# Three stages in one kernel: token weights split under the image attention, the next batch's statistics and first transposes inside the last attention round, projections ahead of half the gates and of the downs

## Chip, cores and metric
One NeuronCore of a Trainium2 chip runs the whole program. The time is the device time of one execution in microseconds (us). Before the change it is 1532.42 us, the median of three runs (1531.77 to 1536.89).

## What is computed
Four images of 256 channels and 32x32 places (1024 tokens of 256) go through three blocks:

```python
x = conv_block(x)            # group norm, 1x1 q, k, v; softmax(q k^T / 16) v over 1024 places; 1x1 p; + x
t = tokens(x)                # (4, 1024, 256)
t = t + attn_block(ln(t))    # rms norm, q and k on the hyperbolic ball (atanh, tanh), v linear,
                             # 8 heads, causal softmax of -|q-k|^2 / sqrt(32), o, residual;
                             # rms norm, silu(gate) * up, down, residual
t = t + moe(ln(t))           # 8 experts, 2 a token, 256 -> 1024 -> 256, gelu
x = from_tokens(t)
```

Every matmul with a 16-bit operand is made of three: weights and activations are split into an fp16 high part and an fp16 rest ("high" and "low"), and high x high, high x low and low x high are summed (`split_product`).

## The kernel before
**Image attention** (`conv_attention`, L282). 32 steps, one for a block of 128 queries: 8 for each of 4 images. In step n TensorE computes the scores of block n (`scores`, L385) and the weighted sum of block n-3 (`weighted`, L397); for images 1 to 3 the projections ("units") come between. VectorE takes the row maximum and forms the low part of the probabilities (L540), ScalarE the exponential (L463) and the high part (L468). SyncE transposes both parts by DMA into four slots (L346, L348), behind them in each step it issues a fill of the routing table with blank rows (L350; 34 fills in all, 32 of them of 1056 KB), and every fourth step a store of the result (L339). GpSimd (POOL) only adds a bias to the input of each image (L507). The token block begins when every queue of this one is done, the fills and stores among them.

**Token block** (`token_block`, L607). Four batches. The front of a batch: layer norm statistics and factors (`statistics`, `norm_factors`, `normalised`), four pairs of transposed token tiles (`h_turned`, `h_high`, `h_low`) with one buffer for the transposed pair and one PSUM bank, the projections to q, k, v tile by tile (`qkv`, `qk_copy`, `v_copy`), the chain of small steps to the ball and to tanh (`length_roots`, `onto_ball`, `logs`, `log_factor`, `qk_roots`, `tangent_length`, `tanhs`, `factors`), then scaling, splitting and stacking q and k into a tile (`scale_qk`, `stack_high`, `stack_low`) that SyncE transposes by DMA (`turn`, L778, 16 transposes a batch). Attention then has 24 steps in four rounds (4, 4, 8 and 8 key blocks): four score matmuls, exp, and sums against v and against ones. Behind it come output projection, second norm, eight gate and up pairs with silu and product (`gate`, `silu`, `ff_product`, `ff_high`, `ff_low`), and four downs (`down`, `add`).

The order on each engine is written out by hand. `attention(b, nb)` holds the rounds with some side work: output for the first half at step 12, the mean of the squares of the first half at 17, the next batch's statistics at 21, the roots of both norms on ScalarE at 22, the factors on VectorE at 23. `late(b, nb)` mixes the rest of batch b with the front of batch b+1: two `h2_turned`, gate 0, output 2 and 3, gate 1, the first transposed pair of the next batch, gate 2, its projections 0 to 5 with gate 3 and the second half's transposes between, down 0, projections 6 and 7, down 1, gates 4 to 7, downs 2 and 3. `last_late` is the late part of the last batch, with no next one. All engines but SyncE run batches 1 and 2 as a loop.

**Token weights** (`weight_strip` on TensorE L955, `weight_high` L1160, `weight_low` L1520). The seven weight matrices of this block are loaded by SyncE (L790) at its start, transposed on TensorE in 18 strips, split by ScalarE and VectorE, in between the steps of the first batch's front. The norm weights' loads (L800) are issued behind the token loads and the first three weights, and VectorE waits for them before anything else (L1633).

**Expert weights** (`split_piece`, L737). POOL splits the experts' weights in 32 pieces of 128x1024: load, scale (L741), high part (L745), low part (L747), two stores. Eight pieces follow the stacking copies (`second_high`, L726) of each of the four batches.

## Time and profile before

| what | us |
| --- | --- |
| median of three runs | 1532.42 |
| the profiled execution | 1548.29 |
| its span, first to last instruction | 1546.5 |

```profile
PE 1217.2 (79%) x9365; PEld 820.5 (53%) x9366; DVE 767.9 (50%) x1460; ACT 702.5 (45%) x1330; POOL 485.7 (31%) x411
PE   3989999452988698869777985440699999999992
PEclk9999999776999899979998996555899999999996
DMA  4576989824630662085108305994433433433326
```

The first line gives each engine's busy time and its share of the span. The other three cut the span in 40 slices of 38.7 us: TensorE's busy share in tenths, the clock that it was granted in tenths of full speed, the mean busy share of the 16 DMA engines. The image attention ends in the eighth slice, the token block runs from there to the 25th, routing to the 27th, then the experts.

### The profile page before, as it was taken

The numbers are of one execution on the slowest core, as the hardware profiler recorded it, in microseconds if no ns is written. First come the engines' busy times: TensorE is split into PE (matmuls) and PEld (weight loads), VectorE is DVE, ScalarE is ACT, GpSimd is POOL, SyncE is SP. The second block draws the span as 40 slices with busy tenths as digits, with TensorE's granted clock in tenths as the row PEclk, the third lists the DMA queues.
The fourth block names the chain that finished last, engine by engine and source line by source line (L and its number), as shares of the span: only waits on it lengthen the run. The fifth ranks groups of instructions, "written<-read, shape, count | busy, mean of one in ns | idle before, by whom it ended". The sixth has DMA issues, their size and how long they took to land. (4 is left out here: it accounts for less than half of the span.)

```text
span 1546.5 us, 27783 instructions
## 1 busy us (share of the span) xinstructions
PE 1217.2 (79%) x9365; PEld 820.5 (53%) x9366; DVE 767.9 (50%) x1460; ACT 702.5 (45%) x1330; POOL 485.7 (31%) x411
## 2 busy tenths in 40 slices
PE   3989999452988698869777985440699999999992
PEld 1546666331334333433343343340588888888882
DVE  3755555156464657556655454542244444444441
ACT  3565454155567666756675652320232332333321
POOL 2021000101960294049305910557032332332331
PEclk9999999776999899979998996555899999999996
DMA  4576989824630662085108305994433433433326
GB/s 136 136 205 183 251 246 234 239 86 77 169 110 8 112 181 82 14 147 168 55 14 168 119 35 149 246 258 136 67 47 53 54 44 51 54 45 51 54 34 224
DMA packets 350675, 183.50 MB, mean 119 GB/s; under 512 B 271104, under 2 KB 337920, under 8 KB 350464
## 3 DMA queue, kind: packets, MB, share of 16 engines
q1 hardware_dynamic: 317056, 124.66, 35.3%
q0 software_dynamic: 25184, 56.64, 15.0%
q10 hardware_dynamic: 8352, 1.08, 0.5%
q8 instruction: 54, 0.88, 0.2%
q14 instruction: 29, 0.24, 0.0%
HBM read 38.66 MB, written 83.11 MB: 79 GB/s over the span
## 5 line engine op out<-in xcount | busy, mean ns | idle before, releaser
L2074 ACT ACTIVATE moe_hid<-moe_hbank,moe_b1T 128x256 f32<-128x256 f32 x312 | 130.2, 471 | 265.5 <-PE moe_hbank L2031 265.5
L2031 PE MATMUL moe_hbank<-moe_xT,l_w1T 128*128 128x256 f16 x1872 | 212.7, 274 | 45.7 <-DMA moe_xT<-rows_scratch 44.4
L2031 PEld LDWEIGHTS moe_hbank<-moe_xT,l_w1T 128*128 x1872 | 183.9, 98 | 68.2 <-issue 46.1
L2010 POOL DMA_INDIRECT acc_scratch<-moe_y,moe_meta x78 | 122.5, 1570 | 310.9 <-DVE moe_y L2101 288.2
L2046 PE MATMUL moe_ybank<-l_w2T,moe_hid_hi 128*128 x1248 | 206.4, 273 | 0.3 <-DVE moe_hid_lo L2088 0.3
L1111 ACT ACTIVATE block_probs<-block_bank 128x1024 f32<-128x1024 f32 (+1 forms) x192 | 144.8, 808 | 81.2 <-PE block_bank L870 67.2
L2046 PE MATMUL moe_ybank<-l_w2T,moe_hid_lo 128*128 x624 | 170.1, 273 | 0.0
L2086 DVE TENSOR_SCALAR moe_hid_hi<-moe_hid 128x2048 f16<-128x2048 f32 x39 | 47.8, 1227 | 203.4 <-ACT moe_hid L2074 203.4
L2046 PEld LDWEIGHTS moe_ybank<-l_w2T,moe_hid_hi 128*128 128x128 f16 x1248 | 122.1, 98 | 14.7 <-issue 0.6
L867 PE MATMUL block_bank<-block_qkT 128*128 128x512 f16 (+3 forms) x384 | 95.6, 338 | 39.6 <-DMA block_qkT<-block_stack 28.3
L732 POOL COPY block_stack<-block_stack 128x512 f16<-128x512 f16 x16 | 11.2, 700 | 315.1 <-ACT block_stack L1095 315.1
L867 PEld LDWEIGHTS block_bank<-block_qkT 128*128 128x128 f16 x384 | 34.2, 99 | 120.6 <-ACT block_probs L1111 68.4
L741 POOL TENSOR_SCALAR block_raw<-block_raw 128x1024 f32<-128x1024 f32 x32 | 90.8, 2838 | 0.7
L2088 DVE SCALAR_TENSOR_TENSOR moe_hid_lo<-moe_hid,moe_hid_hi 128x2048 f16<-128x2048 f32 x39 | 89.4, 2293 | 1.3
L893 PE MATMUL block_bank<-block_probs,block_v 128*32 128x512 f32 (+3 forms) x768 | 84.1, 511 | 5.9 <-ACT block_probs L1111 5.9
L272 PE MATMUL block_bank<-block_qkv,block_hT 128*128 128x256 f16 (+1 forms) x384 | 70.0, 332 | 21.1 <-ACT block_qk L1070 8.4
L893 PE MATMUL block_bank<-block_probs,block_ones 128*32 128x512 f32 (+3 forms) x768 | 80.9, 493 | 0.0
L272 PE MATMUL conv_avx<-conv_v_hi,conv_pt_hi 128*128 128x256 f16 x256 | 72.2, 282 | 8.3 <-DMA conv_pt_lo<-conv_ph_lo 8.3
L540 DVE SCALAR_TENSOR_TENSOR conv_ph_lo<-conv_probs,conv_ph_hi 128x1024 f16<-128x1024 f32 x32 | 39.2, 1224 | 73.0 <-ACT conv_ph_hi L468 73.0
L463 ACT ACTIVATE conv_probs<-conv_score,conv_negmax 128x1024 f32<-128x1024 f32 x32 | 35.6, 1112 | 82.9 <-DVE conv_negmax L535 82.9
L272 PE MATMUL block_bank<-block_down,block_ff_hi 128*128 128x256 f16 x256 | 51.8, 308 | 26.0 <-DVE block_ff_lo L1494 26.0
L272 PE MATMUL conv_avx<-conv_v_hi,conv_pt_lo 128*128 128x256 f16 x256 | 72.2, 282 | 0.0
(354 smaller groups left out, 2550.2 us busy)
## 6 DMA issues: line engine op xcount, KB each, us to landing
rows_scratch<-l_blank SPq DMA_DIRECT2D x32, 1056.0 KB, 5.3
block_raw<-in_L_ffn_w POOLq DMA_DIRECT2D x32, 512.0 KB, 4.6
w_parts<-block_raw_hi POOLq DMA_DIRECT2D x32, 256.0 KB, 4.4
w_parts<-block_raw_lo POOLq DMA_DIRECT2D x32, 256.0 KB, 4.8
l_xs<-in_x SPq DMA_DIRECT2D x8, 512.0 KB, 7.2
x_scratch<-conv_mixed SPq DMA_DIRECT2D x8, 512.0 KB
block_t<-x_scratch SPq DMA_DIRECT2D x16, 256.0 KB, 4.1
acc_scratch<-block_res SPq DMA_DIRECT2D x16, 256.0 KB, 2.2
```

What stands on the lines that cost most here:

```text
L272: last = pe.matmul(out, a, b, start=start and k == 0, stop=stop and k == n - 1)
L540: dve.scalar_tensor_tensor(ph_lo[n % SLOTS][:, :], probs[i % 2][:, :], P_GAIN, ph_hi[n % SLOTS][:, :], ALU.mult, ALU.subtract).then_inc(ph ...
L741: pool.tensor_scalar(raw[q][:, :], raw[q][:, :], GAIN, None, ALU.mult).then_inc(raw_scaled, 1)
L867: last = pe.matmul(bank[:, 2 * (n % 2) + i, q0:512], qkT[:, 1, hh, kb * P:(kb + 1) * P], qkT[:, 0, hh, qh * 512 + q0:(qh + 1) * 512], star ...
L893: last = pe.matmul(out[i * HD:(i + 1) * HD, q0:512], lhs, probs[:, m % 2, i, q0:512], start=kb == 0, stop=kb == last_kb)
L1111: act.activation(probs[:, m % 2, 2 * p:2 * p + 2, q0:512], src, ACT.Exp, scale=SCALE).then_inc(S["exp_done"], 1)
L2010: pool.indirect_dma_start(acc, bass.IndirectOffsetOnAxis(ap=meta[r][:, t, 0:1].bitcast(U32), axis=0), y[r % 2][:, t, :], None, compute_op= ...
L2031: last = pe.matmul(hbank[:, c, :], w1T[:, e, wp, k, c * P:(c + 1) * P], xT[q][:, xp * CC + k, :], start=n == 0, stop=n == 5)
L2046: last = pe.matmul(ybank[q][:, t, :], (hid_hi, hid_lo)[hp][q][:, c, t * P:(t + 1) * P], w2T[:, e, wp, c, :], start=n == 0, stop=n == 3 * H ...
L2074: act.activation(hid[q][:, c, :], hbank[:, c, :], ACT.Gelu, bias=b1T[:, e, c:c + 1], scale=1.0 / (GAIN * GAIN)).then_inc(S["gelu_done"], 1)
L2086: dve.tensor_scalar(hid_hi[q][:, :, :], hid[q][:, :, :], HID_GAIN, None, ALU.mult).then_inc(S["hi_done"], 1)
L2088: dve.scalar_tensor_tensor(hid_lo[q][:, :, :], hid[q][:, :, :], HID_GAIN, hid_hi[q][:, :, :], ALU.mult, ALU.subtract).then_inc(S["lo_done" ...
```

## The change
- The token weights (7 matrices) are loaded in ten chunks of 128x512 in the image attention's steps 14 to 23, split by ScalarE and VectorE in steps 16 to 25, and their parts transposed by DMA (36 transposes) by SyncE in steps 17 to 24, 27 and 28. Strips on TensorE go.
- POOL splits 24 of the 32 pieces of expert weights in the image attention (5 behind the bias adds of image 0, then 2, 4 and 13), and 3, 3 and 2 in batches 0 to 2 of the token block.
- Of the 34 fills, 10 are issued in the image attention (in steps 1, 3, ... 19), 24 in the token block: 8 behind the last turn of batches 0, 1 and 2.
- The token block loads its tokens first, then the norm weights. Two buffers and two PSUM banks for the transposed pair; the attention rounds have buffers of their own for quotient and inverse in place of `h`.
- In the last attention round: next batch's statistics at step 15, mean of squares at 17, both roots at 18, factors at 19, the next batch's first half normalised at 20, first half's transposes (`h2_turned` 0 and 1) at 20 and 22, next batch's first pair at 21.
- `late`: projections 0 to 7 of the next batch come ahead of gates 3 to 7 and of all downs.

```diff
+        chunks = [(u, o, 512 // wt.shape[1]) for u, wt in token_weights for o in range(0, wt.shape[0] // P, 512 // wt.shape[1])]
+        LOAD_AT, SPLIT_AT, TURN_AT = 2 * QB - 2, 2 * QB, (*(2 * QB + 1 + c for c in range(8)), 3 * QB + LAG, 3 * QB + LAG + 1)
...
+                def load_chunk(c):
+                    u, o, k = chunks[c]
+                    if c >= 2:
+                        sp.wait_ge(nat_lo_done, c - 1)
+                    sp.dma_start(nat[c % 2][:, :].rearrange("p (o i) -> p o i", o=k),
+                                 whole[u].rearrange("(o p) i -> p o i", p=P)[:, o:o + k, :]).then_inc(nat_loaded[c % 2], 16)
+
+                def turn_chunk(c):
+                    u, o, k = chunks[c]
+                    sp.wait_ge(nat_lo_done, c + 1)
+                    for i in range(k):
+                        for part, nat_part in zip(token_parts[u], (nat_hi, nat_lo)):
+                            sp.dma_start_transpose(part[:, :, (o + i) * P:(o + i + 1) * P],
+                                                   nat_part[c % 2][:, i * 512 // k:(i + 1) * 512 // k]).then_inc(nat_turned[c % 2], 16)
...
-                    for dst, src in fills[n::STEPS]:
+                    for dst, src in fills[n // 2:n // 2 + 1] if n % 2 else ():
                         sp.dma_start(dst, src).then_inc(filled, 16)
+                    if 0 <= n - LOAD_AT < len(chunks):
+                        load_chunk(n - LOAD_AT)
+                    if n in TURN_AT:
+                        turn_chunk(TURN_AT.index(n))
...
             @block.gpsimd
             def _(pool):
+                ends = (0, 5, 7, 11, EARLY)
+                pieces.load(pool, 0)
+                pieces.load(pool, 1)
                 for b in range(B):
                     for c in range(CC):
                         pool.wait_ge(hn_act, 2 * (b * CC + c) + 1)
                         pool.tensor_scalar(xs[:, b, c, :], xs[:, b, c, :], fold_bias[:, c:c + 1], None, ALU.add).then_inc(x_biased, 1)
+                    pieces.run(pool, ends[b], ends[b + 1], EARLY)
+                pieces.stored(pool, EARLY)
...
+                        if m == ROOT_STEP + 2:
+                            pe.wait_ge(S["attn_done"], b * NR + NR - 1)
+                            h2_turned(b, 0)
+                        if m == ROOT_STEP + 3 and nb is not None:
+                            h_turned(nb, 0)
+                        if m == ROOT_STEP + 4:
+                            pe.wait_ge(S["h2T_lo"], b * PAIRS + 1)
+                            h2_turned(b, 1)
...
                 def late(b, nb):
-                    h2_turned(b, 0)
-                    h2_turned(b, 1)
                     gate(b, 0)
+                    pe.wait_ge(S["hT_lo"], nb * PAIRS + 1)
+                    h_turned(nb, 1)
+                    gate(b, 1)
+                    qkv(nb, 0)
                     output(b, 2)
+                    pe.wait_ge(S["hT_lo"], nb * PAIRS + 2)
                     output(b, 3)
-                    gate(b, 1)
-                    h_turned(nb, 0)
-                    gate(b, 2)
-                    qkv(nb, 0)
                     qkv(nb, 1)
-                    h_turned(nb, 1)
-                    h2_turned(b, 2)
-                    h2_turned(b, 3)
+                    pe.wait_ge(S["o_added"], b * PAIRS + 3)
+                    h_turned(nb, 2)
                     qkv(nb, 2)
                     qkv(nb, 3)
-                    h_turned(nb, 2)
-                    gate(b, 3)
+                    gate(b, 2)
+                    pe.wait_ge(S["o_added"], b * PAIRS + 4)
+                    h2_turned(b, 2)
+                    pe.wait_ge(S["hT_lo"], nb * PAIRS + 3)
+                    h_turned(nb, 3)
                     qkv(nb, 4)
+                    pe.wait_ge(S["h2T_lo"], b * PAIRS + 3)
+                    h2_turned(b, 3)
                     qkv(nb, 5)
-                    h_turned(nb, 3)
-                    down(b, 0)
                     qkv(nb, 6)
                     qkv(nb, 7)
+                    gate(b, 3)
+                    gate(b, 4)
+                    down(b, 0)
                     down(b, 1)
-                    gate(b, 4)
                     gate(b, 5)
                     gate(b, 6)
                     gate(b, 7)
-                    down(b, 2, nb)
-                    down(b, 3, nb)
+                    down(b, 2)
+                    down(b, 3)
```

ScalarE's and VectorE's lists in `late` follow the same order; in VectorE's the two first `add`s move behind `stack_low(nb, 0)` and `ff_product(b, 5)`. The methods of `WeightPieces` hold what `load_piece` and `split_piece` did.

## Rows read from the trace of the kernel before

**Rows 1.** The chain of waits by line.

```profile
DMA out_tok<-acc_scratch 1%; SPq L2135 0%; PE out_bank L2146 0%; ACT out_res L2164 0%; POOL out L2172 0%; POOLq L2171 0%
```

**Rows 2.** Windows: us, PE, PEld, DVE, ACT, POOL busy (count); clock, DMA share, GB/s.

```profile
121.60:245.20 123.60, 123.60 (x840) 82.96 (x839) 70.88 (x129) 64.04 (x97) 5.66 (x2) 1.00 0.86 235
269.70:302.62 32.92, 19.34 (x131) 14.16 (x128) 6.59 (x15) 6.67 (x11) 0.00 (x1) 0.83 0.89 239
302.62:382.14 79.52, 27.34 (x152) 16.84 (x153) 39.54 (x110) 39.13 (x99) 6.90 (x16) 0.67 0.34 90
...
530.70:596.87 66.17, 61.84 (x590) 25.01 (x587) 34.25 (x50) 46.02 (x68) 61.13 (x46) 1.00 0.63 165
596.87:682.63 85.76, 62.39 (x345) 34.98 (x345) 56.29 (x119) 55.12 (x121) 5.67 (x9) 0.90 0.26 51
...
897.30:944.80 47.50, 37.57 (x229) 22.48 (x226) 25.09 (x40) 17.90 (x34) 0.00 (x0) 0.96 0.07 25
```

**Rows 3.** Timeline of the image attention's end; the last two: DMA issues, us to landing.

```profile
273.67 0.38 PE L410 MATMUL conv_avx<-all_ident,l_xs 128*128 128x128 f32 x2
...
278.06 1.22 DVE L540 SCALAR_TENSOR_TENSOR conv_ph_lo<-conv_probs,conv_ph_hi 128x1024 f16<-128x1024 f32 x1 [2.36 <-ACT conv_ph_hi L468]
...
284.71 2.65 SPq L348 DMA_TRANSPOSE conv_pt_lo<-conv_ph_lo  x1
...
290.80 0.28 PE L272 MATMUL conv_avx<-conv_v_hi,conv_pt_hi 128*128 128x256 f16 x1 [2.34 <-DMA conv_pt_lo<-conv_ph_lo]
...
rows_scratch<-l_blank SPq DMA_DIRECT2D x32, 1056.0 KB, 5.3
...
conv_pt_lo<-conv_ph_lo SPq DMA_TRANSPOSE x32, 3.4
```

**Rows 4.** Timeline of the token block's first front and the start of attention.

```profile
302.62 0.90 SPq L770 DMA_DIRECT2D block_t<-x_scratch  x2
...
315.16 2.71 DVE L1278 BATCH_NORM_STATS2 block_stats<-block_t 128x6 f32<-128x256 f32 x8 [18.93 <-DMA block_n<-in_L_attn_norm_w]
...
331.31 0.58 ACT L1070 ACTIVATE block_qk<-block_bank 128x512 f32<-128x512 f32 x1
...
356.32 0.19 ACT L1074 ACTIVATION_READ_ACCUMULATOR block_junk_qk<-block_qk 128x1 f32 x1
...
361.73 0.22 ACT L1084 ACTIVATE block_tc<-block_tb 128x16 f32<-128x16 f32 x1
...
382.14 0.58 PE L867 MATMUL block_bank<-block_qkT 128*128 128x512 f16 x1 [25.82 <-DMA block_qkT<-block_stack]
```

**Rows 5.** ScalarE's waits, 596.87 to 655 (total, times, longest); then its timeline.

```profile
ACT block_qk L1070 <- PE block_bank L272: 6.0, 6, 2.9
ACT block_turned_hi L1153 <- DVE block_h L1445: 4.6, 2, 2.9
ACT block_turned_hi L1134 <- PE block_bank L924: 2.9, 2, 2.2
ACT block_junk L1125 <- DVE block_qk L1464: 2.1, 1, 2.1
...
651.87 0.22 ACT L1084 ACTIVATE block_tc<-block_tb 128x16 f32<-128x16 f32 x1
...
683.38 1.02 ACT L1111 ACTIVATE block_probs<-block_bank 128x1024 f32<-128x1024 f32 x1 [0.41 <-PE block_bank L870]
```

**Rows 6.** POOL's groups by line, 382 to 534 (busy, mean ns); VectorE beside POOL, timeline.

```profile
L741 POOL TENSOR_SCALAR block_raw<-block_raw 128x1024 f32<-128x1024 f32 x9 | 25.9, 2881 | 0.2
L747 POOL TENSOR_TENSOR block_raw_lo<-block_raw,block_raw_hi 128x1024 f16<-128x1024 f32 x8 | 17.4, 2177 | 0.7
L745 POOL CAST block_raw_hi<-block_raw 128x1024 f16<-128x1024 f32 x8 | 8.7, 1088 | 0.5
...
582.55 1.79 DVE L1518 SCALAR_TENSOR_TENSOR block_turned_lo<-block_h,block_turned_hi 128x512 f16<-128x512 f32 x1 [1.79 <-ACT block_turned_hi L1158]
...
732.01 1.64 DVE L1470 TENSOR_SCALAR block_mean_sq<-block_hsq 128x4 f32<-128x4 f32 x1
```

More of the change, by code:

```diff
@@ L2206, in build @@
         ident, ident_h = s.sb("ident", [P, P]), s.sb("ident_h", [P, P], F16)
+        filled = s.sem("filled")
+        front = ExitStack()
+        outer, s = s, Scope(nc, front, "front")
+        pieces = WeightPieces(s, outer, splits)
+        blank = s.sb("blank", [P, GT, ROW], F16)
+        make_blank_rows(nc, blank)
+        blocks_v = rows.rearrange("(n t p) r -> t p n r", p=P, t=GT)
+        fills = [(blocks_v[t][:, n:min(n + 8, BLOCKS), :],
+                  blank[:, t:t + 1, :].bitcast(U32).to_broadcast((P, min(8, BLOCKS - n), ROW // 2))) for n in range(0, BLOCKS, 8) for t in range(GT)]
+        EARLY_FILLS = 10
+        shared = s.sb("shared", [P, B * CC * T * 2], F16)
+        names = ("q", "k", "v", "o", "gate", "up", "down")
+        token_weights = [(n, p[f"L1_attn_{n}_w"]) for n in names]
+        at, parts = 0, {}
+        for n, k, f in (("qkv", CC, 3 * D), ("o", CC, D), ("gate", CC, FF), ("up", CC, FF), ("down", FC, D)):
+            parts[n] = [shared[:, at + i * k * f:at + (i + 1) * k * f].rearrange("p (k f) -> p k f", k=k) for i in range(2)]
+            at += 2 * k * f
+        token_parts = {**{n: [part[:, :, i * D:(i + 1) * D] for part in parts["qkv"]] for i, n in enumerate("qkv")},
+                       **{n: parts[n] for n in names[3:]}}
+        t1 = shared[:, (B - 1) * CC * T * 2:B * CC * T * 2].bitcast(F32).rearrange("p (t d) -> p t d", t=NT)
+        mixed = shared[:, at:at + 2 * 512 * 2].bitcast(F32).rearrange("p (a q) -> p a q", a=2)
         with ExitStack() as ctx:
@@ L2232, in build @@
             first_group_norm(nc, norms[0])
-            conv_attention(nc, xs, x1, scale, shift, norms[1], fills, w, bias, bias_loaded, fold_bias, ident)
+            conv_attention(nc, xs, x1, scale, shift, norms[1], fills[:EARLY_FILLS], w, bias, bias_loaded, fold_bias, ident,
+                           token_weights, token_parts, pieces)
             s.clear()
-        token_block(nc, x1, acc[0:B * T, :], ident, ident_h, [p[f"L1_attn_{n}_w"] for n in ("q", "k", "v", "gate", "up", "down", "o")],
-                    p["L1_attn_norm1_w"], p["L1_attn_norm2_w"], splits)
+        token_block(nc, x1, acc[0:B * T, :], ident, ident_h, parts, t1, mixed, p["L1_attn_norm1_w"], p["L1_attn_norm2_w"], fills[EARLY_FILLS:], filled, pieces)
+        front.close()
         with ExitStack() as ctx:
```

377 lines of the change are left out of this document (176 added, 201 removed).

## The prediction, made before the kernel was run

> **What bounds the kernel now.** I read the chain of waits first, and it says little: it covers only the writing out of the result, a DMA and some transposes worth one or two per cent of the span [rows 1]. The windows by stage say more [rows 2]. From 121.6 to 245.2 us, query blocks 8 to 23 of the image attention, TensorE is busy all 123.6 us: 16 blocks at 7.7 us each, VectorE at 70.9 us (4.4 a block), the DMA engines at 0.86. That stretch is TensorE's. From 269.7 to 302.6 it is busy 19.3 of 32.9 us. From 302.6 to 382.1, the first front of the token stage, it has 27 of 79.5 us, at a clock of 0.67. Attention takes 66 to 67 us a batch with TensorE at 62: again its own. The late part of a batch takes 81 to 86 us with TensorE at 59 to 62, VectorE at 56 and ScalarE at 55 of the 86: no engine is full there, so an order of work and a chain set it. There are three such late parts, and a last one of 47.5 us. The routing and expert stages are not touched.
>
> **Image attention, the tail.** The scores of the last block end before the transpose at 273.7, and VectorE has its low part ready at 279.3 (278.06 + 1.22). SyncE is behind with blank rows, one 1056 KB fill per block, so it issues that transpose only at 284.7, and TensorE starts on it at 290.8, after three such waits [rows 3]. The change leaves 10 fills, all by block 19. Then the transpose is issued at 279.4 and lands 3.4 us later (the median), at 282.8; TensorE has by then done blocks 28 to 30 (273.9 + 3 x 2.8 = 282.3) and ends the last at 285.6 where it ended at 295.1. Minus 9.5. It could be 0 if POOL's DMAs take the room of the fills, and 12 if the waits before go too.
>
> **Image attention, what comes in.** POOL gets 24 of the 32 pieces of expert weights. A piece costs 2.9 + 1.1 + 2.2 us of work [rows 6] and about 1.7 us of issuing and 0.4 of hops, 8.2 us; 24 are 197 us. The last 13 come behind POOL's last bias add, which lies in the window from 121.6 [rows 2]; 13 x 8.2 = 107 us, so from about 141 to about 249, before the end at 286. Cost nothing for their length; if a piece took 11 us they would end where the stage ends. The ten weight chunks add on ScalarE and VectorE one 128x512 pass each per block (0.6 and 0.7 us) and on SyncE 36 small transposes and 10 loads. SyncE issues two large transposes and a fill in about 3.2 us of a 7.7 us block; four more transposes, if each cost the 1.3 us of a large one, make it 8.4: late by 0.7 us a block for eight blocks, 6 us, against the three blocks (23 us) that lie between a transpose and its use. I count 0; the upper end is 3.
> What is not free is that POOL and VectorE get in each other's way. With a POOL instruction running, a VectorE instruction on 4 columns took 1.64 us where it takes 0.17, and ended as POOL's did; the 128x512 low part took 1.79 instead of 0.69 [rows 6]. Not each one is hit: over the token stage's own low parts and small scalings I take a mean of 0.5 us. Three such instructions a block give 4.4 + 1.5 = 5.9 us, with a weight chunk 7.1, still under 7.7. I charge 1.5 us for the stretch before the first block, where VectorE is nearly full. Bounds: 0, and 20.
> The Trainium skill (SBUF — State Buffer, "SBUF: two separate sides") speaks against this part: the pair of ports that VectorE and GpSimd share is an exclusive lock for a whole instruction, not a split of bandwidth. The 1.64 us row agrees. By the rule the sum for this stage would be 0 instead of -8, by the mean of the rows it stays -8; the third rival works that out from the rows.
> Sum for the stage: -9.5 + 1.5 = -8.
>
> **First front.** Now the statistics wait 18.9 us for the norm weights, whose loads stand behind the token loads and three weights, and start at 315.2; then weight strips lie between all steps on three engines; ScalarE reads the first projection at 331.3, the last sum of squares at 356.5, tanh is at 361.7 and attention begins at 382.1 [rows 4]. After: four token loads from 302.6 let the statistics start near 306. Eight statistics, aggregates and small steps (2.7 + 0.6 + 0.9), a root (0.2 + 0.3) and the first half normalised (3.1) give 314; two low parts and the second half (1.4 + 3.1) 319.8; lengths, roots, ball and logs 322.5. Before, the projections' 8 copies with two squares each took 25.2 us because strips stood between them; ScalarE's own part is 1.9 to 2.2 us a tile, so 8 x 2.2 + 1.2 for two high parts = 18.8, ends 341.3. That is 15.1 us earlier than 356.4. The roots then need not wait for a strip nor for VectorE: tanh at 344.2, 17.5 earlier. Behind it nothing is changed: attention starts 20.4 us after tanh as now. Minus 17.5, between 12 and 22. The eight fills issued behind the last turn take some 26 to 35 us of DMA, beside attention, whose DMA share is about 0.6; the next token loads stand behind them and are due some 40 us into it. Cost 0, at most 4 for this batch.
>
> **Attention rounds.** Three groups of four transposes move in here (1.9 us of TensorE for the three), and the table loads for the two roots move from step 22 to step 18, where a step is long enough to hide most of it; a stall like the 1.4 us before the last step goes. Net +0.5 a batch (-1 to +3), with the transposes now standing behind their VectorE inputs two steps later.
>
> **Late part.** Take the middle one, 596.9 to exp at 683.4: 86.5 us [rows 5]. Tanh, which opens scaling and stacking, ends at 652.1, 55.2 us in. ScalarE waited in that time 6.0 + 4.6 + 2.9 + 2.1 = 15.6 us, mostly for projections that stand behind gates 2 and 3 and a down. The change takes 3 high parts (1.8 us) out, leaving about 37.8 us of ScalarE work. It starts when gate 0 is done, some 3.6 us in; walking both lists in order I find waits of another 5 to 6 us (the second half normalised reaches TensorE near 17.6 us where it is free at 13.3). Tanh at 47.5, 7.7 earlier. From tanh to the first exp it was 31.3 us, and stays bound by four scalings, four stackings, four products and low parts on VectorE and by sixteen transposes on SyncE (about 1.4 us each); adds 0 and 1 now come into it and hold SyncE's store before the first turn: +2. Net -5.5 a batch, with the moved work +0.5: -5 x 3 = -15. Bounds per batch: 0, and 11 if only ScalarE's sum counted. TensorE isn't the limit: 13 us of gates and 10.4 us of downs behind the last projection fit in.
> The last late part [rows 2] loses two transposes' time and a wait, 2.7 us, for 1.2 moved: -1.5 (0 to -3).
>
> **Sum.** -8 - 17.5 - 15 - 1.5 = -42. The profiled execution took 1548.3 us (span 1546.5, 1.8 around it): 1506.3. The median of the runs is 15.9 us lower, the stages shrink alike, so 1532.4 - 42 = 1490.
>
> **Rivals.**
> 1. The late part is set by its tail, turns and stacking, wherever tanh lies: gain there +0.5 x 3 - 0, so 1532.4 - 8 - 17.5 - 1.5 + 1.5 = 1507. For: 31 of 86 us lie behind tanh. Against: nothing in that tail waits for anything but itself, so an earlier tanh moves it whole.
> 2. More comes: TensorE's half clock (0.67 in the first front, 0.90 in the late part) is left with its idle time, and late parts give 9: 1532.4 - 8 - 20 - 27 - 3 = 1474. For: the clock rows. Against: the walk finds new waits, which keep the clock down in places.
> 3. The wait is that of an exclusive lock at random times. POOL's three instructions leave a mean rest of (2.9² + 1.1² + 2.2²) / (2 x 8.2) = 0.9 us to each of three VectorE instructions: 7.1 us a block, and 8.7 with a weight chunk, 1.0 over 7.7 for seven to ten blocks: +8, so 1498. The rule that an instruction of either engine holds the ports for its whole length is that of the Trainium skill (SBUF — State Buffer, "SBUF: two separate sides"); by it the time is this 1498.
> 4. Slower than before. In the image attention each such VectorE instruction waits as long as the longest row, 1.47 us: VectorE needs 8.8 us a block, 11 with a chunk, and it paces the stage: +9 for blocks 8 to 15, +26 for 16 to 23, +19 and more in the last eight and +15 in the first (which have 5.4 us a block on TensorE), some 70 in all, with the tail's gain gone: 1532.4 + 70 - 34 = 1568. It decides at a mean wait of 1.15 us. For: POOL would be at work three quarters of the stage. Against: the mean in the token stage is half of that, where POOL is as busy.
> 5. The change gives nothing: fills and pieces only move, and the DMA engines are as full (0.86) with 24 MB of pieces in place of 23 MB of fills, holding transposes and token loads so that both gains at the seams go: 1532.
>
> **Numbers.** Forecast 0.48, rivals 1 to 5: 0.18, 0.12, 0.12, 0.07, 0.03. Range: 1470 to 1513 takes in the forecast, rivals 1 to 3 but for their edges, and the bounds of the front. Within 0.3% (4.6 us, what this kernel's measurement tells from nothing) is only rival 5's neighbourhood. Faster 0.90, same 0.03, slower 0.07.
>
> **What would show it.** The first token load near 294.5; statistics 3 to 4 us behind it; attention starting near 356 and from token load to there 62 us; late parts from last weighing to first exp near 81 us; TensorE still full over blocks 8 to 23 at 7.7 us each. Wrong if a block there takes over 8 us, if TensorE waits for VectorE in it, or if tanh comes later than 50 us into a late part.

## The result: slower by 1.3%, and the profile after

The changed kernel takes 1553.7 us (median of 4 runs, 1551.6 to 1555.1), the kernel before 1534.2 beside it (1531.8 to 1536.9): a ratio of 1.0126, with a 95% interval of 1.0102 to 1.0149. The forecast was 1490, between 1470 and 1513, with 0.07 on slower. It was wrong in sign.

I lay the seams of the stages, the moments at which one ends and the next begins, beside each other first. They are read off the timeline: the pt_hi transposes of query blocks 8 and 31, the first token load, the first score matmul of each batch, its last weighing matmul, and the last down matmul. In us, from the profiled executions:

```
                                       before    after    difference
pt_hi transpose of block 8             121.6     124.3      +2.7
blocks 8 to 31 (that to block 31's)    160.7     196.0     +35.3
from there to the first token load      20.3      17.2      -3.1
first front (to the first score)        79.5      63.9     -15.6
attention, batches 0, 1, 2     66.8 64.0 66.2    76.7 75.5 65.3   +20.5
late parts 0, 1, 2             84.0 85.8 81.5    75.5 77.1 75.5   -23.2
last batch, first score to last down   113.4     117.3      +3.9
end of the downs                       943.6     964.3     +20.7
```

So the parts that I worked out with care came (-15.6 and -23.2), and two others that I had priced at next to nothing cost more: 35 us in the image attention and 9.9 and 11.5 us in two of the attentions. Behind the downs the two executions differ by 14 us the other way (149.1 us to the first expert matmul before, 135.2 after). The change touches nothing there, and over all profiled kernels of this study, the one before among them, that stretch lies between 134 and 153 us: it is a spread of executions, no gain. It goes with the occasion: in the kernels beside which the one before took 1544 or 1546 us, and in the profiled execution of the one before itself (1548), it is 143 to 153 us, in all others 134 to 138.

The windows of after, with the columns of [rows 2]; the first two are the blocks 8 to 21 and the whole stretch from block 8 to block 31, then the first front, attention 0 and 1, the late part 1, attention 2 and the last late part:

```profile
124.30:261.00 136.70, 118.46 (x756) 76.12 (x755) 76.78 (x118) 57.84 (x89) 128.93 (x96) 0.93 1.02 258
124.30:320.30 196.00, 169.55 (x1088) 109.39 (x1086) 106.57 (x175) 84.68 (x131) 129.31 (x96) 0.93 0.91 222
...
337.48:401.40 63.92, 22.91 (x112) 12.61 (x113) 33.35 (x94) 33.09 (x83) 6.64 (x16) 0.66 0.30 70
401.40:478.08 76.68, 66.36 (x580) 25.57 (x580) 35.50 (x61) 46.62 (x70) 24.79 (x19) 0.89 0.66 196
553.55:629.07 75.52, 64.99 (x582) 25.13 (x579) 36.34 (x62) 46.33 (x69) 24.62 (x19) 0.93 0.68 202
629.07:706.19 77.12, 59.36 (x333) 34.44 (x333) 51.92 (x110) 50.78 (x117) 5.02 (x5) 0.91 0.25 45
706.19:771.49 65.30, 61.42 (x580) 24.42 (x580) 30.20 (x56) 43.85 (x66) 12.05 (x10) 1.00 0.62 165
915.00:964.30 49.30, 39.20 (x224) 23.28 (x224) 23.81 (x38) 16.73 (x33) 0.00 (x0) 0.93 0.05 17
```

In the first row TensorE has 118 of 137 us, where it had 123.6 of 123.6 [rows 2]; POOL is at work 129 us, and the DMA share, which adds up the time of all packets and can so pass 1, has gone from 0.86 to 1.02. Who waits for whom stands in the table of waits from 200 to 335 us (in total, times, longest; `conv_nat` is a weight chunk, `conv_probs` and `conv_ph` are the probabilities and their parts):

```profile
ACT conv_nat_hi L548 <- DMA front_shared<-conv_nat_lo: 41.3, 8, 12.6
ACT conv_probs L528 <- DVE conv_negmax L613: 34.7, 14, 3.5
DVE conv_ph_lo L618 <- ACT conv_ph_hi L533: 33.0, 14, 2.4
DVE conv_nat_lo L629 <- ACT conv_nat_hi L548: 32.1, 8, 10.4
PEld conv_prod L272 <- DVE conv_k_lo L604: 16.4, 3, 8.6
PE conv_prod L272 <- DVE conv_k_lo L604: 15.4, 3, 8.4
```

ScalarE stands eight times, 5 us each, in `weight_high`, ahead of the next block's exp, until the transposes of chunk c - 2, which used the same slot (one of the two buffers for a chunk), have landed. The timeline of one such block, SyncE's issues and ScalarE (start, us, engine, line):

```profile
230.33 1.30 SPq L389 DMA_DIRECT2D conv_nat<-in_L_attn_gate_w  x1
231.67 2.69 SPq L397 DMA_TRANSPOSE front_shared<-conv_nat_hi  x1
234.40 1.26 SPq L397 DMA_TRANSPOSE front_shared<-conv_nat_lo  x1
235.70 1.25 SPq L397 DMA_TRANSPOSE front_shared<-conv_nat_hi  x1
236.99 1.30 SPq L397 DMA_TRANSPOSE front_shared<-conv_nat_lo  x1
238.38 1.45 SPq L405 DMA_TRANSPOSE conv_pt_hi<-conv_ph_hi  x1
...
242.11 0.63 ACT L548 ACTIVATE conv_nat_hi<-conv_nat 128x512 f16<-128x512 f32 x1 [7.22 <-DMA front_shared<-conv_nat_lo]
```

A transpose of 128x256 occupies SyncE for 1.25 us, as one of 128x1024 does where nothing holds it (see e13 below); the four small ones of this block are 6.5 us, for the first, behind a fill and a load, takes 2.69. Blocks 17 to 24, from one pt_hi transpose to the next, take 8 to 15 us each, 11.3 in the mean. Over blocks 8 to 31 the transposes of the probabilities themselves land in 4.4 us at the median where they took 3.0 before.

The two long attentions. SyncE's and VectorE's timeline in batch 0, and TensorE's wait that follows:

```profile
407.66 4.10 SPq L828 DMA_TRANSPOSE block_qkT<-block_stack  x3
411.81 28.38 SPq L833 DMA_DIRECT2D rows_scratch<-front_blank  x8
440.23 6.36 SPq L811 DMA_DIRECT2D front_shared<-x_scratch  x4
...
450.07 2.87 DVE L1303 BATCH_NORM_STATS2 block_stats<-front_shared 128x6 f32<-128x256 f32 x8 [7.42 <-DMA front_shared<-x_scratch]
...
458.80 0.63 ACT L1200 ACTIVATE block_turned_hi<-front_shared 128x512 f16<-128x512 f32 x1 [6.16 <-DVE front_shared L1543]
...
463.44 0.61 PE L906 MATMUL block_bank<-block_qkT 128*128 128x512 f16 x1 [7.74 <-ACT block_probs L1147]
```

The eight fills hold SyncE for 28.4 us. The token loads come at 440.2, the statistics at 450.1, 48.7 us into the attention, and `normalise(2)` (L1543, the quotient of the round before) behind them on VectorE is late: ScalarE waits 6.2 us for it and TensorE 7.7. In batch 2, where two of the eight fills are small, the statistics start 38.4 us in, and TensorE's wait at that place is 1.7 us.

### The profile page after: what moved, and what is told of

The parts are those of the page before. It is cut to its first block and busy times, and to the rows that moved or that the text cites. A ratio compares the mean times of both kernels' runs of the same rounds, so it can differ in the third digit from the quotient of the medians.

```text
span 1552.4 us, 27639 instructions
## 1 busy us (share of the span) xinstructions
PE 1228.1 (79%) x9325; PEld 824.1 (53%) x9326; DVE 768.9 (50%) x1454; ACT 693.0 (45%) x1318; POOL 490.2 (32%) x411
## 5 line engine op out<-in xcount | busy, mean ns | idle before, releaser
L300 POOL TENSOR_SCALAR front_raw<-front_raw 128x1024 f32<-128x1024 f32 x32 | 91.3, 2853 | 0.6
L272 PE MATMUL block_bank<-block_turned_hi,front_shared 128*128 128x512 f16 x256 | 80.1, 379 | 8.3 <-DVE block_turned_lo L1514 5.5
L618 DVE SCALAR_TENSOR_TENSOR conv_ph_lo<-conv_probs,conv_ph_hi 128x1024 f16<-128x1024 f32 x32 | 50.7, 1584 | 72.1 <-ACT conv_ph_hi L533 72.1
L272 PE MATMUL block_bank<-front_shared,block_hT 128*128 128x256 f16 (+1 forms) x384 | 77.5, 356 | 10.9 <-ACT block_qk L1106 6.2
L272 PE MATMUL block_bank<-front_shared,block_ff_hi 128*128 128x256 f16 x256 | 58.9, 335 | 29.8 <-DVE block_ff_lo L1525 29.8
L306 POOL TENSOR_TENSOR front_raw_lo<-front_raw,front_raw_hi 128x1024 f16<-128x1024 f32 x32 | 73.3, 2290 | 2.7
```

The costliest lines, as they stand in the source:

```text
L272: last = pe.matmul(out, a, b, start=start and k == 0, stop=stop and k == n - 1)
L300: pool.tensor_scalar(self.raw[q][:, :], self.raw[q][:, :], GAIN, None, ALU.mult).then_inc(self.scaled, 1)
L306: pool.tensor_tensor(self.lo[q][:, :], self.raw[q][:, :], self.hi[q][:, :], ALU.subtract).then_inc(self.lo_done, 1)
L618: dve.scalar_tensor_tensor(ph_lo[n % SLOTS][:, :], probs[i % 2][:, :], P_GAIN, ph_hi[n % SLOTS][:, :], ALU.mult, ALU.subtract).then_inc(ph ...
```

## The experiments

The theories at the start. T1: the image attention is longer because ScalarE waits for the chunks' slots. T2: the attentions are longer because the fills stand ahead of the token loads. The rivals: POOL and VectorE are in each other's way (R1), and the moved statistics themselves (R2). T3, that POOL's transfers keep the loop's transposes waiting, came out of the first four runs.

What each kernel showed, in us (blocks 8 to 31; first token load; attentions 0, 1, 2; last down), and its ratio to the kernel before on the same chip:

```
              blocks   load   attentions        down    median  ratio (95%)
before        160.7   302.6   66.8 64.0 66.2    943.6
after         196.0   337.5   76.7 75.5 65.3    964.3   1553.7  1.0126 (1.0102-1.0149)
e1_spread     183.4   323.7   76.4 75.4 65.3    947.9   1551.9  1.0067 (1.0037-1.0098)
e2_fills      196.2   336.5   69.8 69.9 65.3    946.0   1554.0  1.0064 (1.0030-1.0099)
e3_both       186.5   329.0   69.4 68.6 65.3    940.9   1542.1  0.9967 (0.9931-1.0002)
e4_slots      183.9   330.8   76.7 75.8 66.5    953.8   1559.2  1.0089 (1.0055-1.0123)
e5_late       158.3   292.8   70.5 69.4 68.5    906.1   1499.9  0.9770 (0.9728-0.9812)
e6_dma        191.3   353.0   70.5 69.5 68.5    966.2   1558.0  1.0152 (1.0116-1.0189)
e7_pool       160.1   298.7   70.5 70.8 68.6    915.6   1507.3  0.9822 (0.9787-0.9857)
e8_nofills    171.1   311.3   69.4 68.5 66.6    924.3   1517.8  0.9893 (0.9866-0.9921)
e9_after_late 174.4   310.1   88.5 88.4 78.4    968.4   1552.6  1.0118 (1.0097-1.0139)
e10_last      158.3   295.9   70.5 71.3 69.1    912.8   1503.4  0.9784 (0.9759-0.9809)
e11_chunks    174.3   310.8   70.5 71.4 68.8    924.5   1518.2  0.9908 (0.9887-0.9928)
e12_fills16   162.4   298.1   72.9 71.1 68.5    910.5   1502.2  0.9811 (0.9785-0.9838)
e13_slots4    166.7   303.7   70.5 69.2 68.4    919.1   1525.1  0.9856 (0.9771-0.9940)
```

The runs were made on several chips: beside e1 to e4 the kernel before took 1544.0, beside e13 1546.1, beside the others 1533 to 1534. Medians of different rows compare only through the ratios; the stages, which differ far less from chip to chip, carry the argument. How far one profiled execution can be trusted is seen in e5 and e10, which have the same code up to the last batch: their 23 blocks agree to 0.1 us, their first token loads differ by 3.1.

**e1_spread.** The chunks come every second block.

```diff
-        LOAD_AT, SPLIT_AT, TURN_AT = 2 * QB - 2, 2 * QB, (*(2 * QB + 1 + c for c in range(8)), 3 * QB + LAG, ...)
+        LOAD_AT, SPLIT_AT, TURN_AT = QB, QB + 2, tuple(QB + 3 + 2 * c for c in range(10))
```

> Against the changed kernel (1553.7 us) only the steps of the image attention move at which the ten weight chunks are loaded, split and turned: every second step from 8, 10 and 11 on instead of every step from 14, 16 and 17 on. The same work, but a slot is reused three steps after its transposes were issued instead of one. Theory T1 (ScalarE waits in order for a slot's transposes, because SyncE cannot issue four small transposes and two large ones in every step): steps 17 to 24 fall from 11 to 13 us to 8 or less, the first token load comes at 337 - 30 = 307 us (between 303 and 315), the kernel at 1524. Rival R1 (GpSimd's scalings and VectorE's longer operations in the image attention): the same work beside it, so the first token load stays at 330 or later and the kernel at 1545 to 1554.

The first token load came 14 us earlier, not 30: neither T1's 307 nor R1's 330. The slots' schedule is a part; the load is still 21 us behind that of the kernel before.

**e2_fills.** The fills of a batch stand behind the next batch's token loads.

```diff
-                fill(0)
                 for b in range(1, B):
                     for pr in range(PAIRS):
                         load(b, pr)
+                    fill(b - 1)
...
-                    if b < B - 1:
-                        fill(b)
```

> Against the changed kernel only the place of the eight fills of a batch in SyncE's queue moves: behind the token loads of the next batch instead of ahead of them. Theory T2 (the fills hold SyncE for 28.4 us, so that the statistics of the next batch stand 48 us into the attention and what follows them on VectorE is late for the end of the round): attention 0 and 1 go from 76.7 and 75.5 us back to 65 to 67, the kernel to 1554 - 20 = 1534. Rival R2 (the statistics themselves, or the second norm ahead of them, lengthen the attention wherever the loads stand): attention 0 and 1 stay within 3 us of 76, the kernel at 1548 to 1554.

T2 holds for the larger part: the attentions fall by 6.9 and 5.6 us to 69.8 and 69.9, not to the 65 to 67 expected, and the last down comes 18.3 us earlier, of which 12.5 stand in them, 3.2 in the late parts and 1.3 in the last batch. The ratios (1.0064 against 1.0126) show 9.5 us, half of that and half of the 20 expected; why the rest isn't seen there is open. R2 keeps a remainder: 3 to 6 us in each of the two attentions over the kernel before stay wherever the loads stand.

**e3_both.** Both edits.

> Both edits. If T1 and T2 hold and are independent, 1554 - 30 - 20 = 1504, some 2% below the kernel before. If the two share a cause (one resource, such as the queue's landing time), less than the sum: 1515 to 1525.

The ratio of 0.9967 is 1529 us beside a kernel before of 1534.2, as the changed kernel's 1553.7 was measured: neither 1504 nor 1515 to 1525. T2's part came, of T1's a part again.

**e4_slots.** Four slots instead of two, at the steps of the change.

```diff
-        nat = [s.sb(f"nat{i}", [P, 512]) for i in range(2)]
+        nat = [s.sb(f"nat{i}", [P, 512]) for i in range(4)]
```

> The changed kernel with four slots for the raw chunk and its two halves instead of two, at the steps of the changed kernel. It parts T1 in two. T1a (only the reuse of a slot after one step): with four slots ScalarE no longer waits for the turning of a slot, the image attention gets back nearly all of 30 us, the kernel at 1524 to 1528. T1b (SyncE's issue time itself): at 1.25 us an issue a step has two large and four small transposes, 7.5 us, half a fill of 3.5 us and a load, 9.5 us or more against a block of 7.3; over eight steps 2 to 3 us each stay, 16 to 24 in all, and only 6 to 14 us come back: 1540 to 1548.

Twelve of the 35 us come back in the 23 blocks (the profiled execution lost 6 before block 8 already), as T1b has it; T1a is out. Each of the two edits on the chunks, e1's and this one, leaves 23 us over the kernel before. What the waits show in e4 is TensorE waiting for `conv_pt_lo` (13.8 us in 5 waits between 150 and 310 us), and the median time to landing of that transpose, 125 to 285 us: 3.3 before, 5.6 after, 6.7 in e1. So T3.

**e5_late, e6_dma, e7_pool.** No piece in the image attention; then the transfers of 24 pieces alone added there; then POOL's arithmetic alone.

```diff
-                    pieces.run(pool, ends[b], ends[b + 1], EARLY)
-                pieces.stored(pool, EARLY)
...
-                late_ends = (EARLY, EARLY + 3, EARLY + 6, *(len(pieces.splits) for _ in range(2)))
+                late_ends = tuple(len(pieces.splits) * b // B for b in range(B + 1))
```

> e3_both without any piece of the experts' weights in the image attention: all 32 run in the token block, eight a batch, as in the kernel before. With e3_both the image attention took from the pt_hi transpose of block 8 (126.2 us) to that of block 31 (312.8) 186.6 us, against 160.7 before, and transposes landed in some 6 us against 3.2. Theory T3 (POOL's queue keeps the 16 DMA engines, which were 93% busy before, from the transposes of the loop): without its 16 MB the 23 blocks take 160 to 166 us and the first token load comes at 303 to 309. Rival T1c (SyncE's own issues, two small transposes a step more, are what is left): 180 us or more stay. The late parts take the pieces back: their time and the kernel's go from 1542 to between 1515 (nothing given back) and 1545 (all of it given back).

> e5_late with the transfers of 24 pieces added in the image attention, one piece a block, and none of POOL's arithmetic: 512 KB in and twice 256 KB out, from tiles that hold ones, over the places that the token block's own pieces write later. T3 with the transfers as the cause: the 23 blocks take as long as in e3_both, 180 us or more. If it is POOL's arithmetic beside VectorE's: as in e5_late.

> e5_late with POOL's three operations a piece added in the image attention for 24 pieces, one piece a block, on tiles that nothing loads and nothing stores. Transfers as the cause: as e5_late within 3 us. POOL beside VectorE as the cause: ph_lo's mean stays at 1.4 us or more instead of 1.22, the steps are longer by 0.4 us or more each, 10 us or more over 23 blocks.

T3 is shown. Without the pieces the 23 blocks take 158.3 us and the kernel 1499.9, 2.3% below the one before, better than either bound of the expectation. The transfers alone bring 191.3 back (e6's pieces are paced by the blocks, and it lost 26 us before block 8 too); the arithmetic alone brings 160.1, with a limit that follows below. The rows of e5 for the blocks and the first front, columns as above:

```profile
118.14:276.42 158.28, 157.88 (x1088) 107.46 (x1086) 94.66 (x175) 84.74 (x131) 5.81 (x2) 1.00 0.74 171
292.81:356.40 63.59, 22.62 (x112) 12.60 (x112) 33.37 (x94) 33.08 (x82) 6.90 (x16) 0.66 0.31 71
```

TensorE is full and at full clock again, and the DMA engines at 0.74. The late parts took the eight pieces a batch back at no cost: 74.9, 74.4 and 74.6 us.

The arithmetic is not without trace, and the groups by line show where. VectorE's low part of the probabilities, which reads two tiles in SBUF, from before, after, e6 and e7 (busy, mean ns):

```profile
L540 DVE SCALAR_TENSOR_TENSOR conv_ph_lo<-conv_probs,conv_ph_hi 128x1024 f16<-128x1024 f32 x32 | 39.2, 1224 | 73.0 <-ACT conv_ph_hi L468 73.0
L526 DVE SCALAR_TENSOR_TENSOR conv_k_lo<-conv_prod,conv_qk_bias,conv_k_hi 128x512 f16<-128x512 f32 x10 | 7.3, 745 | 1.1 <-ACT conv_k_hi L455 1.1
```

```profile
L618 DVE SCALAR_TENSOR_TENSOR conv_ph_lo<-conv_probs,conv_ph_hi 128x1024 f16<-128x1024 f32 x31 | 49.5, 1595 | 69.8 <-ACT conv_ph_hi L533 69.8
L604 DVE SCALAR_TENSOR_TENSOR conv_k_lo<-conv_prod,conv_qk_bias,conv_k_hi 128x512 f16<-128x512 f32 x10 | 7.3, 743 | 1.3 <-ACT conv_k_hi L520 1.3
```

```profile
L637 DVE SCALAR_TENSOR_TENSOR conv_ph_lo<-conv_probs,conv_ph_hi 128x1024 f16<-128x1024 f32 x29 | 35.5, 1225 | 66.5 <-ACT conv_ph_hi L534 66.5
```

```profile
L632 DVE SCALAR_TENSOR_TENSOR conv_ph_lo<-conv_probs,conv_ph_hi 128x1024 f16<-128x1024 f32 x32 | 43.1, 1347 | 72.6 <-ACT conv_ph_hi L534 72.6
```

In the mean it is 0.37 us longer in after and 0.12 in e7, not at all in e6, while the low parts of k, which read the projection from PSUM, take 0.74 us in before and after alike. The mean hides two kinds: in after, single low parts take up to 2.64 us, and the others their 1.22. VectorE has the room for that: 107 us busy of 196. e7 tests this more weakly than it seems. Its pieces wait for `ph_hi_done`, so POOL starts a piece at a fixed place of each block, and what is hit there is rather the low part of a weight chunk: over its pieces' time `conv_nat_lo` takes 1.46 us in the mean of seven and 0.69 without POOL (e11). The arithmetic at the times of the change, without its transfers, was not run; that the transfers alone are enough is e6's result and does not hang on it.

**e8_nofills.** e3 with no fill in the image attention.

```diff
-        EARLY_FILLS = 10
+        EARLY_FILLS = 0
```

> e3_both with the ten fills of the image attention moved into the token block, where 11 or 12 then follow each batch's token loads. By T3 (the DMA engines' capacity, whoever asks): ten fills at 3.1 us of all engines are 31 us less, and the 23 blocks fall from 186.6 to 165 us or so, the kernel from 1542 to some 1525, if the attentions lose no more than 2 us each. If only POOL's queue and not SyncE's fills hurts: 180 us or more stay.

15 us come, not 21. With e10 and e12 below it tells what the price hangs on. The DMA tables over blocks 8 to 31 (packets, MB, share of 16 engines; then the median time to landing), of before and of e8:

```profile
DMA packets 73882, 38.98 MB, mean 243 GB/s; under 512 B 48270, under 2 KB 73870, under 8 KB 73870
...
q1 hardware_dynamic: 73870, 38.82, 92.1%
...
conv_pt_hi<-conv_ph_hi SPq DMA_TRANSPOSE x23, 3.0
```

```profile
DMA packets 70476, 37.35 MB, mean 218 GB/s; under 512 B 61008, under 2 KB 66128, under 8 KB 70462
...
q1 hardware_dynamic: 65600, 20.46, 61.0%
q0 software_dynamic: 4862, 16.71, 35.3%
...
conv_pt_hi<-conv_ph_hi SPq DMA_TRANSPOSE x24, 5.0
```

About the same bytes, engines 92 and 96% busy, and transposes that land in 3.0 us in the one and 5.0 in the other. The same tables over the blocks 8 to 31 of the other kernels (share of the 16 engines that SyncE's queue and POOL's took, in per cent; fills; median landing of `conv_pt_hi`, us; the 23 blocks, us):

```
              SyncE's  POOL's  fills  landing  blocks
before          92.0      0      23     3.0    160.7
e12_fills16     80.5      0      11     3.0    162.4
e5_late         73.2      0       6     3.0    158.3
e10_last        72.3      0       6     2.7    158.3
e7_pool         69.9      0       6     2.8    160.1
e11_chunks      65.1      0       6     2.7    174.3
after           64.0     26.4     6     4.4    196.0
e6_dma          68.2     31.6     6     4.8    191.3
e3_both         71.2     31.0     6     4.9    186.5
e8_nofills      61.0     35.3     0     5.0    171.1
```

In the kernels without POOL's transfers the landing is 2.7 to 3.0 us, from 65 to 92% of the engines, and in those with them 4.4 to 5.0 (of the others, e9 and e13 have 2.7 without them, e1 5.1, e2 4.4 and e4 3.8 with them). The change itself has 90.4% in the sum, less than the kernel before. Before, every byte came from SyncE's own queue: a fill was issued behind a block's transposes and had a block's time to drain. POOL's pieces come from a queue of their own, at any time, and the loop's transposes share the engines with them. The landings are measured; that the order of one queue makes the difference is my reading of them, and pieces issued from SyncE's own queue were not tried. Nor does the landing alone set the time: e8 has the longest one and blocks that are 15 us shorter than e3's.

**e9_after_late, e11_chunks.** The change with nothing undone but the pieces; and e5 with the chunks at the change's steps (its diff is e1's, reversed).

> The changed kernel with one part of it undone: no pieces in the image attention, eight a batch in the token block as before; chunks and fills as in the change. If the pieces' transfers are what fed both SyncE's late transposes and ScalarE's wait for a slot, the 23 blocks fall from 196.0 us to 158 to 163 and the kernel to 1554 - 36 = 1518 or less; the two attentions with the fills ahead of their loads stay at 75 to 77. Rival (the chunks' two slots hold ScalarE by themselves): the 23 blocks stay at 172 or more and the kernel at 1530.

> e5_late (1499.9 us) with the chunks back at the steps of the change, every step from 14, 16 and 17 on; the fills stay behind the token loads. It parts the chunks' schedule from the fills' place: the slot theory without the pieces beside it says 158.3 + 5 to 10 us for the 23 blocks; the transfer theory says that the transposes land in 3 us again, so that the schedule is worth 2 us or less.

Two misses of mine. The pieces are worth 27.4 us to the first token load (337.5 to 310.1), but with no transfer of POOL's beside them the chunks still cost 16 us: 174.3 us against 158.3, with transposes landing in 2.7 us. That is the rival's side of e9's expectation. And e9 as a whole gains nothing, for its attentions take 88.5, 88.4 and 78.4 us: now pieces and fills run together, ahead of the token loads. SyncE's and VectorE's timeline in e9's batch 0, with the wait that ends in TensorE:

```profile
384.61 31.53 SPq L829 DMA_DIRECT2D rows_scratch<-front_blank  x8
416.18 9.98 SPq L807 DMA_DIRECT2D front_shared<-x_scratch  x4
...
430.64 1.46 DVE L1299 BATCH_NORM_STATS2 block_stats<-front_shared 128x6 f32<-128x256 f32 x4 [15.16 <-DMA front_shared<-x_scratch]
...
449.51 0.61 PE L902 MATMUL block_bank<-block_qkT 128*128 128x512 f16 x1 [20.98 <-ACT block_probs L1143]
```

A wait of 21 us at the end of a round, where after has 7.7. Behind the loads (e11) the same fills beside the same pieces bring no such wait: the last down comes 43.9 us earlier. The fills' place is thus worth 18 us in the change and 44 with the pieces where they were before.

**e13_slots4.** e11 with four slots, on what the 16 us are.

> e11_chunks (174.3 us for the 23 blocks, transposes landing in 2.7 us, nothing from POOL's queue beside them) with four slots for a chunk instead of two. If what is left of the chunks' price is the wait for a slot after one step, the 23 blocks fall to 158 to 162. If it is SyncE's issue time (two large and four small transposes at 1.25 us, 7.5 us, and half a fill and a load in a block of 7), the eight steps stay above 8 us each: 168 to 174.

```profile
205.56 1.25 SPq L405 DMA_TRANSPOSE conv_pt_hi<-conv_ph_hi  x1
206.86 1.31 SPq L407 DMA_TRANSPOSE conv_pt_lo<-conv_ph_lo  x1
208.22 1.70 SPq L409 DMA_DIRECT2D rows_scratch<-front_blank  x1
209.96 0.58 SPq L389 DMA_DIRECT2D conv_nat<-in_L_attn_gate_w  x1
210.59 2.65 SPq L397 DMA_TRANSPOSE front_shared<-conv_nat_hi  x1
213.27 1.26 SPq L397 DMA_TRANSPOSE front_shared<-conv_nat_lo  x1
214.57 1.25 SPq L397 DMA_TRANSPOSE front_shared<-conv_nat_hi  x1
215.86 1.25 SPq L397 DMA_TRANSPOSE front_shared<-conv_nat_lo  x1
217.21 1.25 SPq L405 DMA_TRANSPOSE conv_pt_hi<-conv_ph_hi  x1
```

In this timeline of SyncE there is no gap in a block of 11.7 us: it is SyncE's issue time, the 2.65 us of the first small transpose included. The blocks 17 to 24 take 9.5 us each with two slots and with four; the four let ScalarE run ahead, and 7.6 us of 16.0 come back behind the chunks. That is between my two expectations, on the side of the issue time.

**e10_last.** In e5, both transposes of the last half stand ahead of gate 3 again, pair 3 in a bank of its own.

```diff
                     h2_turned(b, 2)
+                    h2_turned(b, 3)
                     gate(b, 3)
-                    pe.wait_ge(S["h2T_lo"], b * PAIRS + 3)
-                    h2_turned(b, 3)
                     gate(b, 4)
```

> e5_late with the last late part's two transposes of the second half side by side again ahead of gate 3, pair 3 in bank 4. From the last batch's first score to the end of its downs e5_late takes 117.3 us against 113.4 before; 2.2 us is a wait ahead of gate 4. With it gone: 115 us or so, the kernel 1498. If the wait only moves to the downs: 117.

The last batch took 114.1 us against 117.3 in e5; its late part alone (from the last weighing matmul) takes 45.4 against 49.3, and 46.9 before. TensorE's wait ahead of gate 4 is 2.18 us in after and 0.25 in e10, as before. The row of after:

```profile
934.78 0.39 PE L272 MATMUL block_bank<-block_turned_hi,front_shared 128*128 128x512 f16 x1 [2.18 <-DVE block_turned_lo L1514]
```
In the medians (ratios 0.9784 and 0.9770) nothing of 3 us can be seen; the two kernels can't be told apart.

**e12_fills16.** e10 with 16 fills in the image attention.

> e10_last with 16 fills in the image attention instead of 10, so 6 a batch in the token block. The image attention's DMA engines are 73% busy in e5_late and six fills of 3.1 us are 19 us more, 12% of 160: if the capacity has room to 93%, as before, nothing is lost there (within 2 us), and the attentions gain at most 1 us each: 1496 to 1500. If the transposes wait again: 5 us or more are lost in the 23 blocks.

4.1 us more in the 23 blocks, between my two expectations, and as a whole the same as e10. These blocks hold eleven fills where e10 has six, at 80.5% of the engines: the five more, about 5 MB, cost 4 us with the landing at 3.0, while 16.7 MB from POOL's queue cost e3 28 us, twice as much for each MB.

The best version is e5_late or e10_last: the change with the pieces back in the token block, the chunks every second block and the fills behind the token loads, 2.2 to 2.3% below the kernel before, 3.5% below the changed one by the ratios (0.9770 / 1.0126 = 0.965).

## Why the prediction was wrong, step by step

Two of its own signs of error came true: blocks of over 8 us, and TensorE waiting for VectorE in them (15.4 us for `conv_k_lo` in the table of waits). The first was a poor sign: single blocks of before already lie 8.4 and 9.1 us apart. The third did not come: tanh comes 42.3 us into the late part 1 (671.4 - 629.1), earlier than the 47.5 of the walk.

**Weight chunks on SyncE** failed: "late by 0.7 us a block for eight blocks, 6 us, against the three blocks (23 us) that lie between a transpose and its use. I count 0; the upper end is 3." Its price of one was right (1.25 us, but for the first behind a fill), its surroundings were not. I took 7.7 us for a block where the window of [rows 2] held the 17 blocks 8 to 24, 7.3 us each; I left out the ten loads and the stores; and above all I compared SyncE's lateness with the wrong slack. The three blocks lie between a transpose of the probabilities and its use. The chunk's own reuse of a slot had one block. Over the 23 blocks that is 16.0 us without the pieces (e11 to e5) and 12.5 beside them (after to e1).

**Pieces of the experts' weights** failed in the same sentence as rival 5 had it right: I priced what POOL's pieces do to VectorE, and let their 16 MB stand under "it could be 0 if POOL's DMAs take the room of the fills". What they cost is the landing of the transposes in the loop: 27.4 us to the first token load (e9), 28 in e3's blocks (e5). The arithmetic adds 2 us to the 23 blocks where it was run by itself (e7). Rival 5 spoke of the same engines, but only of gains lost at the seams, and "the DMA engines are as full" was its argument. That was near (0.90 in the 23 blocks of after, 0.92 before) and not the point: as full from SyncE's queue alone, they let the transposes land in 3.0 us.

**VectorE beside POOL**: I charged 0.5 us to each of three instructions a block and 1.5 us to the stage. In the table above one instruction a block is longer, by 0.37 us in the mean; over the blocks beside which POOL is at work (up to 260 us) it is 1.83 us in place of 1.22, 0.6 longer, so the size was near and the number of instructions was not. The arithmetic in e7 costs 1.9 us over the 23 blocks and 5.9 to the first token load (against e5; against e10, the same code up to there, 2.8). Rivals 3 and 4 have the wrong mechanism; rival 4 had the right sign, for the wrong reason, and at 35 us of its 70. By the Trainium skill (SBUF — State Buffer, "SBUF: two separate sides") the shared ports are an exclusive lock, which a VectorE instruction takes in a two-port mode or with two inputs in SBUF, and not otherwise. In these blocks the rows agree as far as they go: the instructions that read two tiles in SBUF are longer, those with a source in PSUM are not. That is one instruction a block, and not three. What the rule would make of the time was not what decided.

**Tail of the image attention**: -9.5 predicted, -3.1 seen from block 31 on. In e5 the first token load comes at 292.8 and in e10 at 295.9, against the 294.6 of the sum: the -8 of the whole image attention was there, at -9.8 and -6.7, once pieces and chunks stand elsewhere.

**First front**: -17.5 predicted, -15.6 came (-15.9 in e5). Right, on its own steps: the statistics start 2.7 us behind the first token load (340.13 - 337.48), where it said 3 to 4.

**Fills and token loads** failed: "Cost 0, at most 4 for this batch." I had the 26 to 35 us of the fills (28.4 came) and the 40 us at which the loads are due, and added neither landing nor the statistics' length: 48.7 us in, on an engine whose next instruction ends a round. It cost 18.3 us by the last down (e2). The change itself moved the statistics ahead of `normalise(2)`; what is queued behind a wait that grows is what I should have named.

**Attention and late parts together**: -5 a batch predicted. In e5 the three late parts are 27.4 us shorter and the three attentions 11.4 longer: -16, against -15. Singly both terms were off, and that their sum agrees is luck: the moved work costs an attention 2.3 to 5.4 us, not 0.5, and a late part gains 7 to 11.

**Last late part**: -1.5 predicted, +2.4 came (49.3 us against 46.9; the other 1.5 of the last batch's +3.9 lie in its attention). What I missed is the order of its second half: the last transpose behind gate 3 brings a wait of 2.2 us ahead of gate 4, and with both ahead of gate 3 (e10) this part takes 45.4 us, the -1.5 predicted.

With these placements undone the kernel's last down stands 37.6 us ahead of the one before (e5), against the -42 of the sum, and its time at 1500 against the 1490 forecast. The sum was nearly that of another kernel, and the nearness is in part luck: in it the attentions, off by 10 us, and the late parts, off by 11 the other way, cancel.

## What to carry to other kernels

Price a moved transfer twice: by its own queue (what stands behind it, and what the waiting engine has queued behind that), and by who else needs the DMA engines in the same microseconds; this loop, which turns tiles through DMA, lived with engines that were 92% busy from its own queue, and lost 28 us to a second queue beside it. For each buffer, compare the producer's lateness with the distance to that buffer's own reuse, not to another's. When a change is worth 40 us in some stages and loses 60 in others, lay the stage seams of both traces side by side before any theory: three small edits turned 1.3% slower into 2.3% faster.

## What the runs showed of the hardware

- The issue of a DMA transpose takes SyncE 1.25 us for 128x256 in 16-bit as for 128x1024; a load or a fill takes 0.58 us where the fills are a block apart, and 3.5 us a fill of 1056 KB when eight stand in a row, while the engines move 343 GB/s, POOL's pieces included (after, 411.8 to 440.2 us). The first small transpose behind a fill and a load took 2.65 us (e11, e13), behind a load alone 1.18.
- With about the same bytes in the same stretch (39.0 and 37.4 MB), transposes landed in 3.0 us when all transfers came from SyncE's queue (92% of the engines) and in 5.0 when 16.7 MB came from POOL's (96% with it).
- In the image attention POOL's arithmetic lengthened only VectorE's operations with two sources in SBUF (1224 to 1595 ns in the mean for 128x1024, single ones to 2640); those with a source in PSUM kept their 743 to 745 ns. In the token block one with a single source in SBUF, on 128x4, took 1.64 us too [rows 6].
- e7's arithmetic, as much of it as the change's (some 100 us in the 23 blocks), lengthened the same low parts to 1347 ns only and hit `conv_nat_lo` instead (691 to 1456 ns): what is hit depends on where in the block POOL starts.
- What is left open: the spread of 134 to 153 us between the last down and the first expert matmul, and the 26 us that e6 lost before block 8.
